# A value convolution's oldest tap as diagonal products on TensorE, and a new order by odd and even slots

## The chip, the cores and the metric

The kernel runs on one core of one Trainium2 chip, as one launch. The metric is device time in microseconds (us); the kernel before takes 1670.02 us (median of 3 runs, 1666.37 to 1673.09). The engines are TensorE (PE; its weight loads are PEld), VectorE (DVE), ScalarE (ACT), GpSimd (POOL) and SyncE (SP, which here issues DMAs). Each runs its own instructions in the order written, and they meet only at semaphores.

## The reference, cut to what matters

```python
# x: (2, 2048, 256); 16 heads of 64 channels; all float32
q, k, v = x @ Wq.T, x @ Wk.T, x @ Wv.T
q, k, v = (causal_depthwise_conv(y, w, b) for ...)  # per channel: b + sum over 4 taps w[tap] * y[t - 3 + tap]
g, beta = log_sigmoid(x @ Wg.T), sigmoid(x @ Wb.T)
k = k / norm(k);  q = q / 8
# per token and head, in order of time (gated delta rule):
#   Sk = S^T k;  S = exp(g) * S + beta * k (v - Sk)^T;  o = S^T q
x = layernorm(x + o @ Wo.T)
x = layernorm(x + routed_experts(x) + shared_expert(x))   # 64 experts, 6 a token
```

The change touches only the convolution of v and the order of the work on the delta rule.

## The kernel before, in words

Three phases follow each other: the gates (to about 57 us), the delta rule (to about 1120 us) and the mixer with its experts. The change is in the delta rule.

**Macros and slots.** The delta rule is cut into 64 macros (`NM`): one pair of heads and a span of 256 tokens, of both sequences. A macro holds 4 chunks of 64 tokens. A loop of 71 slots (`SLOTS`) is written out by hand for every engine; slot t works on several macros at once: macro t (`m`) is projected, macro t-1 (`before`) is convolved, turned and multiplied, macro t-5 (`mi`) has its triangular matrix inverted, and the chain over time (the state S) of a group of two macros advances by two steps, `one` and `two_`. A group's four steps take two slots, so odd and even slots differ: odd slots hold step 0, which needs the finished inverse, and the start of the small 16x16 inverses (`begin_blocks`, `join_fours`), even slots their end (`join_eights`).

**Values.** The projected values land in one PSUM bank `p_j`. ACT copies them to `hist` (channels on partitions, 3 older tokens ahead of each 64) and writes tap 3 and the bias into `yv` (`last_tap`, L796). DVE adds taps 2, 1 and 0 with `conv_values` (L615), each a scalar-times-tensor-plus-tensor over 128x512; each adds one to the semaphore `conv_v`. PE then turns `yv` into tokens on partitions with transposes (`turn_values`, L432), for chunks 0 and 1 and, after `chain_update` and `exponents`, for chunks 2 and 3; `turned` tells ACT, which squares the keys (L810, for DVE's `lengths`, L632) and copies keys and values on (L813).

**Inverse.** Four products in `p_i` (all L464 on PE) alternate with DVE's subtractions `horner` (L703): `inverse_r`, `inverse_rx`, `inverse_ry1`, `inverse_ry2`. The last `horner` is `tt_out`; `inverse_r` of the next macro and the step 0 of the chain wait for it. `inverse_r` also waits for `xd`, which comes by way of a store to memory and a load back (L333, L342, L347 on SP).

**Chain.** `chain_state` (L498, L508), DVE `residual` (L711), `chain_solve` (L523), ACT `solved` (L825), `chain_update` (L535, L544), DVE `update` (L719). `products` (L455) fills all of `p_xy`, and DVE's `mask` (L644) reads it.

**Order around the change.** On PE a slot begins with `chain_state` and the key projection and ends with the query projection, `inverse_ry1`, `products`, `inverse_ry2`. On DVE it begins with the last `horner` of the previous slot's macro, then `residual`, value taps 1 and 0, query taps 2 and 1, `update`, query tap 0, `gate`, `lengths`; it ends with `update`, key taps, value tap 2, `horner`, `mask`.

Of the kernel before, what the change touches and what calls it, by code (L numbers as in the profile page):

```python
# [14 lines left out]
NPAIR = H // 2  # L15
NTOK = NB * T
NTILE = NTOK // 128
C = 64
# [7 lines left out]
CH = 3 + C  # L26
HIST = 8 * CH
# [1 line left out]
RUN = PIECES * C  # L29
UNIT = C // SUB * LANE  # L30
REGION = 32 * UNIT
WCOLS = 2 * 3 * 128
E, K, CAP, I = 64, 6, 128, 176
IA, IB = 112, 64
SI = 2 * I
# [9 lines left out]
def view(t, offset, *dims, parts=None):  # L45
    row = t[:, :].ap[0][0]
    first, count = parts or (0, t.shape[0])
    return bass.AP(t, first * row + offset, [[row, count], *[list(d) for d in dims]])


def half(i):
    return (64 * i, 64)
# [161 lines left out]
def delta_phase(nc, a, s):  # L214
# [5 lines left out]
    with ExitStack() as own:  # L220
# [14 lines left out]
        yv = two("yv", 512)  # L235
# [36 lines left out]
        def is_macro(m):  # L272
            return 0 <= m < NM
# [121 lines left out]
        def _(pe):  # L395
            def project(m, n, done):
                e = m % 2
                if n == 1 and m == 0:
                    pe.wait_ge(tap_k, 1)
                if n == 1 and m >= 1:  # L400
                    pe.wait_ge(exped, m)
                if n == 2:
                    pe.wait_ge(tap_v, m + 1)
                if n == 0:
                    if m >= 1:
                        pe.wait_ge(tap_q, m)
                    pe.wait_ge(w_in[e], 16 * (m // 2 + 1))
                    if m % NPAIR == 0:
                        pe.wait_ge(xt_in[m // 8 % 2], 16 * (m // 16 + 1))
                for ch in range(2):  # L410
                    mm = pe.matmul(p_j[:, :], w[e][:, (ch * 3 + n) * 128:(ch * 3 + n) * 128 + 128],  # L411
                                   xt[m // 8 % 2][:, ch * 512:ch * 512 + 512], start=ch == 0, stop=ch == 1)
                mm.then_inc(done, 1)
# [12 lines left out]
            def turn_values(m, chunks):  # L426

                e = m % 2
                pe.wait_ge(conv_v, 3 * m + 3)
                for c in chunks:  # L430
                    for h in range(2):
                        mm = pe.transpose(view(p_xy, h * 512 + 256 + c * C, (1, C)), view(yv[e], c * 128, (1, 128), parts=half(h)),  # L432
                                          view(const, C_ID + 64 * h, (1, C), parts=half(h)))
                if chunks[-1] == 3:
                    mm.then_inc(turned, 1)

# [113 lines left out]
            for t in range(SLOTS):  # L550
                m, before, mi = t, t - 1, inverse_macro(t)
                one, two_ = chain_step(t, 0), chain_step(t, 1)
                if one:
                    chain_state(*one)
                if is_macro(m):
                    project(m, 0, proj_k)
                if one:
                    chain_solve(*one)
                if is_macro(before):
                    turn_keys(before)  # L560
                    turn_values(before, (0, 1))
                if one:
                    chain_update(*one)
                if is_macro(before):
                    exponents(before)
                if is_macro(before):
                    turn_values(before, (2, 3))
                if is_macro(mi):
                    inverse_r(mi)
                if two_:  # L570
                    chain_state(*two_)
                if is_macro(m):
                    project(m, 1, proj_v)
                if two_:
                    chain_solve(*two_)
                if is_macro(mi):
                    inverse_rx(mi)
                if two_:
                    chain_update(*two_)
                if is_macro(m):  # L580
                    project(m, 2, proj_q)
                if is_macro(mi):
                    inverse_ry1(mi)
                if is_macro(before):
                    products(before)
                if is_macro(mi):
                    inverse_ry2(mi)

        @block.vector
        def _(ve):  # L590
# [14 lines left out]
            def conv_values(m, tap):  # L605

                e = m % 2
                out = view(yv[e], 0, (C, 8), (1, C))
                if tap == 2:
                    ve.wait_ge(carried, m + 1)  # L610
                    ve.wait_ge(tap_v, m + 1)
                else:
                    ve.wait_ge(conv_v, 3 * m + 2 - tap)
                column = (m % NPAIR * 3 + 2) * (TAPS + 1) + tap
                ve.scalar_tensor_tensor(out, view(hist[e], HIST + tap, (CH, 8), (1, C)),  # L615
                                        cw[:, column:column + 1], out, ALU.mult, ALU.add).then_inc(conv_v, 1)
# [106 lines left out]
            for t in range(SLOTS):  # L723
                m, before, mi = t, t - 1, inverse_macro(t)
                one, two_ = chain_step(t, 0), chain_step(t, 1)
                small_group = (t - 3) // 2
                odd, even = t % 2 == 1 and 0 <= small_group < NG, t % 2 == 0 and 0 <= small_group < NG
                if is_macro(mi - 1):
                    horner(mi - 1, ry2_done, 48, tt_out)
                if one:  # L730
                    residual(*one)
                if is_macro(before):
                    conv_values(before, 1)
                    conv_values(before, 0)
                    conv(before, 1, tap_q, conv_q, (2, 1))
                if one:
                    update(*one)
                if is_macro(before):
                    conv(before, 1, tap_q, conv_q, (0,))
                    gate(before)  # L740
                    lengths(before)
                if even:
                    join_eights(small_group, 0, "products")
                if is_macro(m) and t % 2:
                    conv(m, 0, tap_k, conv_k, (2,))
                if is_macro(before):
                    inverse_lengths(before)
                if two_:
                    residual(*two_)
                if even:  # L750
                    join_eights(small_group, 0, "sums")
                    join_eights(small_group, 1, "products")
                    join_eights(small_group, 1, "sums")
                if is_macro(m) and t % 2:
                    conv(m, 0, tap_k, conv_k, (1, 0))
                if odd:
                    begin_blocks(small_group)
                    join_fours(small_group)
                if is_macro(m) and t % 2 == 0:
                    conv(m, 0, tap_k, conv_k, (2,))  # L760
                if is_macro(mi):
                    horner(mi, rx_done, 16, y1_out)
                if two_:
                    update(*two_)
                if is_macro(m) and t % 2 == 0:
                    conv(m, 0, tap_k, conv_k, (1, 0))
                if is_macro(m):
                    conv_values(m, 2)
                if is_macro(mi):
                    horner(mi, ry1_done, 32, y2_out)  # L770
                if is_macro(before):
                    mask(before)

        @block.scalar
# [145 lines left out]
        def _(po):  # L920
# [56 lines left out]
            for t in range(SLOTS):  # L977
                m, before, mi = t, t - 1, inverse_macro(t)
                one, two_ = chain_step(t, 0), chain_step(t, 1)
                if is_macro(before):  # L980
                    po.wait_ge(conv_v, 3 * before + 1)
                if one:
                    decay_state(*one)
                if is_macro(mi):
                    off_diagonal(mi)
                if is_macro(m):
                    carry_in(m)
                if is_macro(before):
                    carry_out(before)
                if is_macro(t - 2):  # L990
                    roots(t - 2)
                if is_macro(before):
                    po.wait_ge(gated, before + 1)
                if two_:
                    decay_state(*two_)
                if is_macro(before):
                    clip(before)
                    factors(before)
                    if t % 2 and t >= 3:
                        po.wait_ge(inverted, STEPS * ((t - 3) // 2) + 11)  # L1000
                    if t % 2 == 0 and is_macro(m):
                        po.wait_ge(conv_k, 3 * m + 1)
                    weight(before)
# [664 lines left out]
```

## Time and profile before

| | |
|---|---|
| profiled execution, whole | 1670.89 us |
| its span, first to last instruction | 1669.1 us |
| PE busy | 1459.8 us (87%) |
| DVE busy | 1202.0 us (72%) |
| ACT busy | 895.3 us (54%) |
| POOL busy | 808.5 us (48%) |
| DVE, L615, value taps, x192 | 150.9 us, 786 ns of one |
| DVE, L602, key and query taps, x384 | 294.8 us, 768 ns of one |
| mean granted TensorE clock | 0.959 of 2.4 GHz |

The shares are averages over three phases with different limits. In the delta rule alone both PE and DVE are busy for over nine tenths of the time. A matmul's end is modelled, so its busy time hides short waits; starts are exact. Each float32 matmul of the program is two instructions (a transpose one), so a call with 8 products shows as x16. "<-" names the instruction that ended an engine's wait.

### The profile page before, as it was taken

To read this page: it belongs to the slowest core of one execution; us is meant where nothing else is said; L and a number is where in the kernel's file an instruction comes from. 1 tells how busy PE (TensorE), PEld (TensorE's weight loads), DVE (VectorE), ACT (ScalarE), POOL (GpSimd) and SP (SyncE) were. 2 spreads that over 40 slices of the span, in tenths; PEclk is the share of its full clock that TensorE was granted. 3 is DMA by queue.
4 is the path that set the end of the run, shared out by engine and by line. 5 is a ranking of instruction groups with operands and counts; after the bars stand their busy time and mean duration, and the time that the engine had idled before them with its cause. 6 is when DMAs were issued, how large, how long until landed. Compare 5 with 4: busy or idle time off the path is not lost. (4 is left out here: it accounts for less than half of the span.)

```text
span 1669.1 us, 62375 instructions
## 1 busy us (share of the span) xinstructions
PE 1459.8 (87%) x25360; PEld 1060.4 (64%) x25360; DVE 1202.0 (72%) x2714; ACT 895.3 (54%) x2506; POOL 808.5 (48%) x1042
## 2 busy tenths in 40 slices
PE   6678999999999999999999999759999997988970
PEld 6235666666666666666666666658899986766650
DVE  1589999999999999998989999524666664323325
ACT  1367777777777777876777777310111110323333
POOL 1133444344344344344334344213777777777775
PEclk9879999999999999999999999788999999999995
DMA  8335555565655655655655565427666521899658
GB/s 321 91 80 119 130 121 128 142 124 131 138 121 134 137 120 134 138 117 131 140 119 128 128 122 127 93 67 228 187 177 187 181 72 37 237 255 254 122 85 309
DMA packets 529133, 242.69 MB, mean 145 GB/s; under 512 B 430000, under 2 KB 495536, under 8 KB 527952
## 3 DMA queue, kind: packets, MB, share of 16 engines
q1 hardware_dynamic: 376176, 198.43, 44.4%
q10 hardware_dynamic: 134208, 21.25, 7.0%
q0 software_dynamic: 18464, 19.03, 6.4%
q8 instruction: 201, 3.29, 0.8%
q14 instruction: 84, 0.69, 0.1%
HBM read 167.13 MB, written 71.50 MB: 143 GB/s over the span
## 5 line engine op out<-in xcount | busy, mean ns | idle before, releaser
L411 PE MATMUL delta_p_j<-xt,w 128*128 128x512 f32 x768 | 395.2, 638 | 22.6 <-ACT delta_yv L796 8.6
L602 DVE SCALAR_TENSOR_TENSOR delta_kq<-delta_hist,cw,delta_kq 128x512 f32<-128x512 f32 x384 | 294.8, 768 | 15.5 <-ACT delta_kq L796 10.6
L973 POOL TENSOR_TENSOR delta_sd<-state,eg_end 128x256 f32<-128x256 f32 x128 | 79.9, 624 | 385.2 <-DVE delta_kqg L625 252.4
L786 ACT ACTIVATE delta_hist<-delta_p_j 128x512 f32<-128x512 f32 x192 | 115.5, 602 | 222.1 <-PE delta_p_j L411 218.7
L411 PEld LDWEIGHTS delta_p_j<-xt,w 128*128 128x128 f32 x768 | 134.3, 195 | 141.9 <-issue 104.5
L1486 POOL DMA_INDIRECT slot_tokens<-tokens,mix_slot x192 | 190.0, 989 | 61.8 <-issue 52.5
L960 POOL TENSOR_TENSOR ex<-ex,delta_bp 128x512 f32<-128x512 f32 x64 | 68.0, 1063 | 188.5 <-DVE delta_xi L682 110.7
L615 DVE SCALAR_TENSOR_TENSOR delta_yv<-delta_hist,cw,delta_yv 128x512 f32<-128x512 f32 x192 | 150.9, 786 | 5.2 <-ACT delta_yv L796 2.9
L857 ACT ACTIVATE delta_kpv<-delta_kpv,delta_root 128x64 f32<-128x64 f32 x512 | 137.2, 360 | 0.0
L523 PEld LDWEIGHTS delta_p_c<-delta_r,delta_kkq 64*64 64x64 f32 x2048 | 71.5, 137 | 102.6 <-issue 52.7
L851 ACT ACTIVATE delta_kpv<-delta_kpv,delta_fk 128x64 f32<-128x64 f32 x512 | 129.0, 346 | 0.0
L464 PEld LDWEIGHTS delta_p_i<-delta_kkq,rt 64*32 64x32 f32 (+1 forms) x4096 | 67.6, 100 | 92.0 <-DVE delta_kkq L703 88.4
L1390 DVE SCALAR_TENSOR_TENSOR wo<-wo,mix_p_h 112x256 f32<-112x256 f32 x64 | 27.0, 421 | 136.2 <-ACT wo L1448 131.1
L1253 PE MATMUL mix_p_h<-wo,w 128*112 128x128 f32 (+1 forms) x768 | 101.9, 283 | 18.9 <-ACT wo L1442 18.6
L1253 PEld LDWEIGHTS mix_p_h<-wo,w 128*112 128x112 f32 (+1 forms) x768 | 89.6, 183 | 42.4 <-ACT wo L1442 36.5
L1509 POOL DMA_INDIRECT acc<-mix_ot,mix_places x64 | 100.6, 1572 | 31.3 <-issue 17.8
L464 PE MATMUL delta_p_i<-delta_kkq,rt 64*32 64x32 f32 (+1 forms) x4096 | 81.5, 184 | 32.5 <-DVE delta_kkq L703 32.5
L967 POOL TENSOR_TENSOR delta_root<-delta_n,half_power 128x8 f32<-128x8 f32 x64 | 106.6, 1666 | 0.0
L1416 ACT ACTIVATE mix_es<-mix_p_g,mix_negmax 128x64 f32<-128x64 f32 x32 | 10.1, 314 | 176.6 <-DVE mix_negmax L1316 176.6
L796 ACT ACTIVATE delta_kq<-delta_p_j,cw 128x512 f32<-128x512 f32 x128 | 100.3, 783 | 0.0
L523 PE MATMUL delta_p_c<-delta_r,delta_kkq 64*64 64x64 f32 x2048 | 89.1, 227 | 10.2 <-DVE delta_r L711 7.3
L644 DVE TENSOR_TENSOR delta_kkq<-delta_p_xy,ex 128x1024 f32<-128x1024 f32 x64 | 78.2, 1222 | 22.9 <-PE delta_p_xy L455 21.9
(171 smaller groups left out, 3345.7 us busy)
## 6 DMA issues: line engine op xcount, KB each, us to landing
delta_xd<-x_scratch SPq DMA_DIRECT2D x256, 128.0 KB
w<-in_wqkv SPq DMA_DIRECT2D x64, 384.0 KB, 3.8
w<-in_w SPq DMA_DIRECT2D x64, 352.0 KB, 3.8
delta_eg<-eg_rows SPq DMA_DIRECT2D x128, 130.0 KB, 3.0
n_scratch<-delta_kkq ACTq DMA_DIRECT2D x128, 128.0 KB, 3.1
ot<-o SPq DMA_DIRECT2D x128, 128.0 KB, 3.0
xt<-ot SPq DMA_DIRECT2D x8, 1024.0 KB
mix_ot<-ot SPq DMA_DIRECT2D x8, 1024.0 KB
```

The source lines that it names most:

```text
L411: mm = pe.matmul(p_j[:, :], w[e][:, (ch * 3 + n) * 128:(ch * 3 + n) * 128 + 128], xt[m // 8 % 2][:, ch * 512:ch * 512 + 512], start=ch == ...
L464: mm = pe.matmul(view(p_i, g * C + first, (1, count), parts=(64 * sh, rows)), view(lhs, g * C, (1, rows), parts=half(sh)), view(rhs, at + ...
L523: mm = pe.matmul(view(p_c, h * 512 + 128 + q * C, (1, C), parts=half(b)), view(kkq, ring(group * 2 + q) + h * 256 + c * C, (1, C), parts=h ...
L602: ve.scalar_tensor_tensor(out, view(hist[e], i * 2 * HIST + tap, (CH, 8), (1, C)), cw[:, column:column + 1], out, ALU.mult, ALU.add).then_ ...
L615: ve.scalar_tensor_tensor(out, view(hist[e], HIST + tap, (CH, 8), (1, C)), cw[:, column:column + 1], out, ALU.mult, ALU.add).then_inc(conv ...
L786: ac.activation(view(hist[e], n * HIST + 3, (CH, 8), (1, C)), view(p_j, 0, (C, 8), (1, C)), ACT.Copy)
L851: ac.activation(kpv[:, at:at + C], kpv[:, at:at + C], ACT.Copy, scale=fk[:, g:g + 1]).then_inc(kp_out, 1)
L857: ac.activation(kpv[:, at:at + C], kpv[:, at:at + C], ACT.Copy, scale=root[m % 2][:, g:g + 1]).then_inc(vp_out, 1)
L967: po.tensor_tensor(root[m % 2][:, :], n2[:, :], view(s.half_power, 0, (0, 8)), ALU.pow).then_inc(small, 1)
L1253: mm = pe.matmul(p_h[e % 2][0:count, to:to + 128], s.w13[:, at * 704 + ch * SI + first:at * 704 + ch * SI + first + count], xbt[e % 2][:, ...
L1486: po.indirect_dma_start(out=s.tok.ap(), out_offset=bass.IndirectOffsetOnAxis(ap=slot[i % 2][:, k:k + 1], axis=0), in_=tokens[:, i:i + 1], ...
L1509: po.indirect_dma_start(out=s.acc[e % 2].ap(), out_offset=bass.IndirectOffsetOnAxis(ap=places[:, e:e + 1], axis=0), in_=yb[e % 4], in_offs ...
```

## The change

- DVE's value tap 0 goes: `conv_values(before, 0)` is not called, and `conv_v` counts 2 a macro.
- PE does it instead. The weights of tap 0 come as two 64x64 diagonal matrices in 64 more columns of the projection weights (`WCOLS` 768 to 832). After the transposes of two chunks, 8 products of `hist` (as stationary operand, shifted to tap 0) with the diagonal accumulate on the turned values in PSUM.
- `inverse_ry2` moves from the end of a slot to the next slot: ahead of the key projection in odd slots, behind it in even ones.
- `products` goes ahead of `inverse_ry1` in odd slots.
- On DVE the last `horner` moves behind `residual` (odd) or behind query taps 2 and 1 (even); query tap 0 moves ahead of `update`; `mask` goes ahead of the second `horner` in odd slots.

```diff
-WCOLS = 2 * 3 * 128
+WCOLS = 2 * 3 * 128 + C
...
             def turn_values(m, chunks):
-                pe.wait_ge(conv_v, 3 * m + 3)
+                pe.wait_ge(conv_v, 2 * m + 2)
                 for c in chunks:
                     for h in range(2):
-                        mm = pe.transpose(view(p_xy, h * 512 + 256 + c * C, (1, C)), view(yv[e], c * 128, (1, 128), parts=half(h)),
-                                          view(const, C_ID + 64 * h, (1, C), parts=half(h)))
+                        pe.matmul(view(p_xy, h * 512 + 256 + c * C, (1, C)), view(yv[e], c * 128, (1, 128), parts=half(h)),
+                                  view(const, C_ID + 64 * h, (1, C), parts=half(h)), is_transpose=True, start=False, stop=False,
+                                  skip_group_check=True)
+                for c in chunks:
+                    for b, h in QUADS:
+                        mm = pe.matmul(view(p_xy, h * 512 + 256 + c * C, (1, C), parts=half(b)),
+                                       view(hist[e], HIST + (c * 2 + b) * CH, (1, C), parts=half(h)),
+                                       view(w[e], 768, (1, C), parts=half(h)), start=False, stop=True, skip_group_check=True)
...
 # PE, a slot
                     chain_state(*one)
+                if is_macro(mi - 1) and t % 2:
+                    inverse_ry2(mi - 1)
                 if is_macro(m):
                     project(m, 0, proj_k)
+                if is_macro(mi - 1) and t % 2 == 0:
+                    inverse_ry2(mi - 1)
...
                     project(m, 2, proj_q)
+                if is_macro(before) and t % 2:
+                    products(before)
                 if is_macro(mi):
                     inverse_ry1(mi)
-                if is_macro(before):
+                if is_macro(before) and t % 2 == 0:
                     products(before)
-                if is_macro(mi):
-                    inverse_ry2(mi)
...
 # DVE, a slot
-                if is_macro(mi - 1):
-                    horner(mi - 1, ry2_done, 48, tt_out)
                 if one:
                     residual(*one)
+                if is_macro(mi - 1) and t % 2:
+                    horner(mi - 1, ry2_done, 48, tt_out)
                 if is_macro(before):
                     conv_values(before, 1)
-                    conv_values(before, 0)
                     conv(before, 1, tap_q, conv_q, (2, 1))
+                if is_macro(mi - 1) and t % 2 == 0:
+                    horner(mi - 1, ry2_done, 48, tt_out)
+                if is_macro(before):
+                    conv(before, 1, tap_q, conv_q, (0,))
                 if one:
                     update(*one)
                 if is_macro(before):
-                    conv(before, 1, tap_q, conv_q, (0,))
                     gate(before)
...
+                if is_macro(before) and t % 2:
+                    mask(before)
                 if is_macro(mi):
                     horner(mi, ry1_done, 32, y2_out)
-                if is_macro(before):
+                if is_macro(before) and t % 2 == 0:
                     mask(before)
```

The waits of `conv_values` and of POOL on `conv_v` are renumbered from 3 to 2 a macro.

## Rows read from the trace of the kernel before

**Rows 1.** Starts (us) of DVE's gate instruction L625, one a slot, 127 to 1048 us.

```profile
L625 DVE TENSOR_TENSOR delta_kqg<-delta_kq,delta_eg x60: 1224/1225/1226, 127.3 to 1046.6; 128x1024 f32<-128x1024 f32 x60
```

**Rows 2.** Busy us (x instructions): PE, PEld, DVE, ACT, POOL; clock, DMA share, GB/s.

```profile
127.00:1048.00 921.00, 866.86 (x20415) 577.10 (x20411) 856.99 (x1623) 702.55 (x1977) 378.71 (x587) 0.99 0.58 128
```

**Rows 3.** Who waited for whom, 127 to 1048 us: us in total, times, longest.

```profile
PE delta_p_i L464 <- DVE delta_kkq L703: 27.4, 49, 0.9
DVE delta_kkq L644 <- PE delta_p_xy L455: 14.8, 30, 0.7
DVE state L719 <- PE delta_p_c L535: 12.6, 32, 0.7
PE delta_p_i L464 <- DMA delta_xd<-x_scratch: 9.3, 10, 1.3
```

**Rows 4.** Line L615 on DVE, 127 to 1048 us: ns shortest/median/longest.

```profile
L615 DVE SCALAR_TENSOR_TENSOR delta_yv<-delta_hist,cw,delta_yv x177: 744/752/1292, 134.7 to 1043.3; 128x512 f32<-128x512 f32 x177
```

**Rows 5.** Timeline of DVE in an even slot: start us, us, engine, line, [idle before].

```profile
601.58 1.23 DVE L644 TENSOR_TENSOR delta_kkq<-delta_p_xy,ex 128x1024 f32<-128x1024 f32 x1 [0.59 <-PE delta_p_xy L455]
...
603.25 1.53 DVE L615 SCALAR_TENSOR_TENSOR delta_yv<-delta_hist,cw,delta_yv 128x512 f32<-128x512 f32 x2
...
608.50 0.68 DVE L632 TENSOR_REDUCE delta_n<-delta_sq 128x8 f32<-128x512 f32 x1
...
616.53 1.22 DVE L644 TENSOR_TENSOR delta_kkq<-delta_p_xy,ex 128x1024 f32<-128x1024 f32 x1
```

**Rows 6.** Timeline of PE over an even slot and the end of an odd one.

```profile
600.31 1.10 PE L455 MATMUL delta_p_xy<-delta_kq 64*64 64x128 f32 x32
601.34 0.57 PE L464 MATMUL delta_p_i<-delta_kkq,rt 64*16 64x16 f32 x32
...
602.47 1.98 PE L411 MATMUL delta_p_j<-xt,w 128*128 128x512 f32 x4
604.38 0.68 PE L523 MATMUL delta_p_c<-delta_r,delta_kkq 64*64 64x64 f32 x16
604.99 0.46 PE L423 MATMUL delta_p_xy<-const,delta_kq 64*128 64x64 f32 x8
...
605.55 0.46 PE L535 MATMUL delta_p_c<-delta_u,delta_kpv 64*64 64x64 f32 x16
605.83 0.41 PE L544 MATMUL delta_p_d<-delta_kkq,delta_u 64*64 64x64 f32 x16
606.38 0.38 PE L445 MATMUL delta_p_j<-arg_r,arg_l 118*128 118x512 bf16 x1
...
615.06 1.10 PE L455 MATMUL delta_p_xy<-delta_kq 64*64 64x128 f32 x32
616.66 0.49 PE L464 MATMUL delta_p_i<-delta_kkq,rt 64*16 64x16 f32 x26 [0.50 <-DVE delta_kkq L703]
...
623.82 1.98 PE L411 MATMUL delta_p_j<-xt,w 128*128 128x512 f32 x4
625.92 0.68 PE L523 MATMUL delta_p_c<-delta_r,delta_kkq 64*64 64x64 f32 x16
...
630.57 0.69 PE L464 MATMUL delta_p_i<-delta_kkq,rt 64*32 64x32 f32 x32 [0.65 <-DVE delta_kkq L703]
```

**Rows 7.** Timeline of ACT in the even slot.

```profile
605.46 0.78 ACT L796 ACTIVATE delta_kq<-delta_p_j,cw 128x512 f32<-128x512 f32 x1
...
607.55 0.60 ACT L810 ACTIVATE delta_sq<-delta_p_xy 128x512 f32<-128x512 f32 x1
```

**Rows 8.** Timeline of SP's queue: the store of the small inverses, the load back.

```profile
612.59 0.39 SPq L333 DMA_DIRECT2D x_scratch<-delta_xi  x1
617.37 1.28 SPq L342 DMA_DIRECT2D delta_xd<-x_scratch  x2
```

**Rows 9.** Timeline of PE where `xd` is late.

```profile
779.32 1.18 PE L464 MATMUL delta_p_i<-delta_xd,noff 64*64 64x48 f32 x29 [1.30 <-DMA delta_xd<-x_scratch]
```

**Rows 10.** The 5 us after it, columns as in rows 2.

```profile
780.00:785.00 5.00, 5.00 (x74) 3.09 (x69) 4.62 (x14) 2.16 (x8) 1.38 (x4) 0.66 0.52 87
```

**Rows 11.** Timeline of PE in the last slots, which hold chain and inverse alone.

```profile
1083.75 0.57 PE L464 MATMUL delta_p_i<-delta_kkq,rt 64*16 64x16 f32 x32 [0.52 <-DVE delta_kkq L703]
```

More of the change, by code:

```diff
@@ L612, in conv_values @@
                 else:
-                    ve.wait_ge(conv_v, 3 * m + 2 - tap)
+                    ve.wait_ge(conv_v, 2 * m + 2 - tap)
                 column = (m % NPAIR * 3 + 2) * (TAPS + 1) + tap
@@ L980, in _ @@
                 if is_macro(before):
-                    po.wait_ge(conv_v, 3 * before + 1)
+                    po.wait_ge(conv_v, 2 * before + 1)
                 if one:
@@ L1637 @@
                    .reshape(NPAIR, 128, TAPS + 1) for n in "kqv"])
+    diag = np.zeros((NPAIR, 2, C, C), np.float32)
+    diag[:, :, np.arange(C), np.arange(C)] = g["attn_cv_w"][:, 0, 0].reshape(NPAIR, 2, C)
     left, right = exponent_operands()
@@ L1644 @@
         "wg": f(wg),
-        "wqkv": f(wqkv),
+        "wqkv": f(np.concatenate([wqkv, diag.reshape(NPAIR, 128, C)], 2)),
         "x": f(x),
```

## The prediction

> **What bounds the kernel now.** I read the page's busy shares first, then the delta rule alone, since nothing outside it changes. One instruction a slot gives the length of a slot: 60 starts of DVE's gate from 127.3 to 1046.6 us, so 919.3 / 59 = 15.58 us [rows 1]. In that stretch DVE is busy for 857 of 921 us and PE for 867 [rows 2]: 93% and 94%. Neither is far from the bound, so the question is which one waits for which. The table of waits shows both [rows 3]. DVE waits 14.8 us for `products` ahead of `mask` and 12.6 us for the state products ahead of `update`, 27.4 us in 59 slots, 0.46 us a slot. What is left, 15.58 - 0.46 = 15.12 us a slot, is DVE's own content: instructions and the hand-overs between them. One slot agrees: from `mask` at 601.58 to `mask` at 616.53 are 14.95 us in which DVE waits for nobody [rows 5]. So even slots are bound by DVE.
>
> PE shows 27.4 us of waits for `horner` and 9.3 us for the late `xd`, 0.62 us a slot [rows 3]. This is too little, since a modelled matmul end covers the first part of a wait. By starts: from `products` to `inverse_ry2` are 1.03 us where nothing is late (600.31 to 601.34) and 1.60 us where `horner` is (615.06 to 616.66), a wait of 0.57 us beside the 0.50 shown [rows 6]. The same correction of 0.07 us on the 0.65 us ahead of `inverse_ry1` (630.57) gives 0.72 us. Smaller ones show in no wait row: from a projection to `chain_solve` are 2.10 us (623.82 to 625.92) against 1.91 (602.47 to 604.38), so 0.19 us for `residual`; and from `chain_update`'s second half to the exponents are 0.55 us (605.83 to 606.38), where 16 matmuls of that kind take 0.28 (605.55 to 605.83) [rows 6]; of the other 0.27 I take 0.12 as a wait for ACT's `last_tap`, which ends at 606.24 [rows 7], in each slot, and as much for `solved`. An odd and an even slot thus hold 0.57 + 0.72 + 0.19 + 4 x 0.12 = 1.96 us, 0.98 us a slot with `xd` (0.16) partly in it or beside it; I take 1.03. PE's content is 15.58 - 1.03 = 14.55 us. PE is 0.57 us below DVE now. PE's waits are mostly for a late DVE, DVE's for PE's tail: the two hold each other up at the slot's end.
>
> **The change part by part.** *Value tap 0 leaves DVE.* One of three L615 of a slot goes, 0.75 us [rows 4]; two run in 1.53 us [rows 5]. DVE's content becomes 15.12 - 0.75 = 14.37 us.
>
> *Diagonal products come to PE.* Two calls a slot, each 8 products of 64x64 with 64 columns, x16 in the trace. The same shape, with both halves of rows and columns in turn as here, is L535: 16 start within 0.28 us (605.55 to 605.83). The same shape in L523's order, where neighbours share the array half by half, takes 0.61 us (604.38 to 604.99) [rows 6]. The change uses L535's kind of order, so I take 0.28 a call, 0.56 us a slot. Below: the transposes already hand over to 64x64 matmuls, so part of a hand-over may be saved, 0.45 us a slot. Above: 1.22 us a slot, L523's price.
> The Trainium skill speaks against this price: the page "TensorE: Matmul & The Clock Gate", section "Wait — 56ns, not 53.3ns?", says that matmul starts are never closer than about 25 ns however few the columns. By it 16 would take 0.40 us and the slot 0.80, which would take back 14 of the microseconds gained below. The rows show 0.28 us for 16, 17.5 ns each [rows 6]; the trace disagrees, and the trace decides.
>
> PE's content becomes 14.55 + 0.56 = 15.11 us. PE passes DVE (14.37) and becomes the bound. Without the reordering little would be won: 15.11 plus the old waits would be a slower slot than before.
>
> *`inverse_ry2` goes to the next slot.* The same 32 instructions, 0.50 us. Its `horner` now has `chain_state` (0.63 us, 601.84 to 602.47, of which the rows show the end) and in even slots also a projection (1.91 us) as cover, where it had `products` alone and fell short by 0.57 us. With DVE 0.75 us earlier relative to PE, I lay two slots out: `horner` ends 0.3 us or more ahead of PE in both. This wait goes. What is queued behind `inverse_ry2` is later by 0.50 us: in even slots `chain_solve`, so ACT's `solved` and `last_tap`, so the exponents; PE reaches them after 0.61 + 0.30 + 0.55 + 0.28 x 2 us more work of its own, about when ACT is done. I leave 0.1 us there.
>
> *`products` ahead of `inverse_ry1` in odd slots.* It fills the 0.72 us of wait for the `horner` behind `join_fours` with 1.04 us of work that is ready (the queries have been convolved for long). This wait goes too.
>
> *DVE's moves.* `residual` first serves `chain_solve`; the 0.19 us goes. Query tap 0 ahead of `update` uses up 0.73 us that `update` would wait for `chain_update`. New waits on DVE: `lengths` needs the squares (L810), which need `turned`, which is now two calls later, 0.56 us, and in even slots 0.50 more. Before, `lengths` starts at 608.50 and the squares end at 608.15 [rows 5, 7]. In the layout DVE waits 0.35 us there, and for `products` ahead of `mask` 0.2 us. Behind them are queued `join_eights` and the next `residual`. DVE has 15.11 - 14.37 = 0.74 us to spare, so this costs nothing on the path; were the cover gone, it would cost 0.2 us a slot (first rival).
>
> *`xd`.* It is stored after `join_eights` (612.59) and loaded 4.8 us later (617.37) [rows 8]; `inverse_r` is at 622.3. In the layout the store is 0.3 us later and `inverse_r` 0.85 us later from the even slot's start, so the margin grows by 0.5 us. Of 0.16 us a slot I keep 0.08. Where it was 1.30 us late, the granted clock fell to 0.66 in the 5 us behind, i.e. to 1.2 GHz for part of them [rows 9, 10]; this should be seen less. SP's queue is otherwise in the same order; `turned`, for which it waits ahead of loading weights, is a microsecond later, with nine to spare. The weights are 416 instead of 384 KB, a load with as much room: no cost.
>
> *Ramp and end.* Before 127 us slots go by the one bank `p_j` between PE and ACT; nothing gained, nothing lost. After 1048 us `inverse_ry2` behind `chain_state` covers its 0.52 us [rows 11] about as often as `horner` comes later for the chain: between -2 and +2 us, I take 0.
>
> **The sum.** A slot: 15.11 + 0.08 (`xd`) + 0.06 left for ACT and hand-overs = 15.25 us. 59 slots x (15.58 - 15.25) = 19.5 us. The profiled execution took 1670.9 us (span 1669.1), so 1651.4; the median of the runs lies 0.9 below it, so 1650.5, and I forecast **1651 us**.
>
> **The rivals.**
> *ACT takes the wait's place.* PE waits for ACT's tap and exponentials and DVE for the squares, both now behind a later `turned`. For: ACT is busy for 702 of 921 us [rows 2], and in even slots from the key projection to the value projection without a pause. Against: 0.7 us of slack on DVE. At 0.2 us a slot more, 15.45: 1651 + 12 = 1663 us.
> *All of it comes off.* `xd` is never late, the clock doesn't fall, products cost 0.45: the slot is 15.05 us, 59 x 0.53 = 31 us, 1639 us.
> *Slower: PE is the bound, and the products cost as much as L523.* Place: both calls of `turn_values`; price 1.22 us a slot. The slot is 14.55 + 1.22 + 0.14 = 15.91 us, 59 x 0.33 = 19 us more, 1690 us. It decides from 0.89 us a slot on, since 14.55 + 0.89 + 0.14 = 15.58. For: PE is now the bound, so everything added counts in full, a clock at 1.2 GHz too. Against: the row of L535. In part (1.0 to 1.1 us) it gives some 1678 to 1684.
>
> **Chances.** Forecast 0.53 (1644 to 1658), ACT's wait 0.20, all of it 0.15, slower 0.12. Faster by over 0.5% (8 us; about what a measurement tells from no change) is the first and third, 0.68; within 0.5% the second, 0.20; slower 0.12. The range for 8 in 10 takes in the second case and most of the third: 1639 to 1671.
>
> **What would show it.** Right: 2 L615 a slot; the diagonal products as x16 rows about 0.28 us to the next start; no wait of L464 for L703 worth 0.1 us a slot; PE without gaps, DVE with 0.6 to 0.8 us of waits, ahead of L632 and L644; slots of 15.2 to 15.3 us. Wrong: 16 products over 0.45 us; slots of 15.4 with waits of PE for L796 or L804; or DVE still without waits, which would mean that PE wasn't the bound.

## The result and the profile after

The changed kernel takes 1626.28 us (median of 4 runs, 1622.26 to 1629.23) against 1668.28 us (4 runs); the ratio is 0.9742, with a 95% interval of 0.9711 to 0.9774. It is 42 us faster. Forecast were 1651 us, 19 us faster, with a range of 1639 to 1671: the direction was right, the size was half of what came, and the time lies below the range.

The profiled execution took 1626.23 us, its span 1624.4 against 1669.1 us. The gate instruction, one a slot, shows where the 44.7 us are; its line of after answers to [rows 1] (ns shortest/median/longest, first and last start).

```profile
L635 DVE TENSOR_TENSOR delta_kqg<-delta_kq,delta_eg x60: 1216/1218/1225, 122.2 to 1003.8; 128x1024 f32<-128x1024 f32 x60
```

Slots went from 15.58 to (1003.8 - 122.2) / 59 = 14.94 us: 59 x 0.64 = 37.6 us. The ramp ahead of it is 127.3 - 122.2 = 5.1 us shorter, what follows the last gate (622.5 against 620.6) 1.9 us.

In the busy shares of that stretch (columns as in [rows 2]) PE goes from 94 to 99%, which fits PE as the bound. DVE's share hardly moves, from 93 to 92%, though it has a tap less to do.

```profile
127.00:1003.00 876.00, 868.83 (x22181) 599.33 (x22179) 808.97 (x1555) 694.04 (x1960) 386.37 (x583) 1.00 0.62 137
```

Who waited for whom in after, 127 to 1010 us (us in total, times, longest); it answers to [rows 3], which ends at the last gate in the same way.

```profile
DVE delta_n L642 <- ACT delta_sq L824: 20.1, 56, 0.5
DVE state L729 <- PE delta_p_c L541: 13.1, 28, 0.8
DVE delta_kkq L654 <- PE delta_p_xy L461: 9.7, 36, 1.0
PE delta_p_i L470 <- DMA delta_xd<-x_scratch: 2.0, 4, 0.6
PE delta_p_i L470 <- DVE delta_kkq L713: 1.4, 2, 0.8
```

PE's waits for `horner` fell from 27.4 to 1.4 us and those for `xd` from 9.3 to 2.0. DVE now waits for the squares, as laid out in the prediction, and still for `chain_update` ahead of `update`.

The timeline of PE over an even slot of after, from `products` of the odd one to `products` of the even one, then the end of the slot (start us, us, engine, line, operation).

```profile
607.49 1.10 PE L461 MATMUL delta_p_xy<-delta_kq 64*64 64x128 f32 x32
608.52 0.69 PE L470 MATMUL delta_p_i<-delta_kkq,rt 64*32 64x32 f32 x32
609.15 0.46 PE L504 MATMUL delta_p_c<-state,delta_kqg 64*64 64x64 f32 x16
...
609.77 1.98 PE L411 MATMUL delta_p_j<-xt,w 128*128 128x512 f32 x4
611.69 0.57 PE L470 MATMUL delta_p_i<-delta_kkq,rt 64*16 64x16 f32 x32
612.19 0.68 PE L529 MATMUL delta_p_c<-delta_r,delta_kkq 64*64 64x64 f32 x16
...
613.10 0.29 PE L432 MATMUL delta_p_xy<-const,delta_yv 64*128 64x64 f32 x4
613.32 0.46 PE L437 MATMUL delta_p_xy<-w,delta_hist 64*64 64x64 f32 x16
613.60 0.41 PE L541 MATMUL delta_p_c<-delta_u,delta_kpv 64*64 64x64 f32 x16
613.83 0.41 PE L550 MATMUL delta_p_d<-delta_kkq,delta_u 64*64 64x64 f32 x16
...
618.47 0.68 PE L529 MATMUL delta_p_c<-delta_r,delta_kkq 64*64 64x64 f32 x16
618.99 1.02 PE L470 MATMUL delta_p_i<-delta_xd,rt 64*64 64x48 f32 x29
...
620.48 1.98 PE L411 MATMUL delta_p_j<-xt,w 128*128 128x512 f32 x4
622.40 0.69 PE L470 MATMUL delta_p_i<-delta_kkq,rt 64*32 64x32 f32 x32
623.02 1.10 PE L461 MATMUL delta_p_xy<-delta_kq 64*64 64x128 f32 x32
623.95 0.41 PE L504 MATMUL delta_p_c<-state,delta_kqg 64*64 64x64 f32 x16
```

No row has a wait in brackets, where [rows 6] has two. The 16 diagonal products take 0.28 us to the next start (613.32 to 613.60), as priced. The even slot, from one `chain_state` (609.15) to the next (623.95), is 14.80 us of PE's own work: PE is the bound, at less than the 15.11 us that the prediction gave it.

### The profile page after: what moved, and what is told of

The parts are those of the page before. It is cut to its first block and busy times, and to the rows that moved or that the text cites. A ratio compares the mean times of both kernels' runs of the same rounds, so it can differ in the third digit from the quotient of the medians.

```text
span 1624.4 us, 66407 instructions
## 1 busy us (share of the span) xinstructions
PE 1469.7 (90%) x27408; PEld 1091.4 (67%) x27408; DVE 1157.5 (71%) x2650; ACT 895.3 (55%) x2506; POOL 819.7 (50%) x1042
## 5 line engine op out<-in xcount | busy, mean ns | idle before, releaser
L411 PE MATMUL delta_p_j<-xt,w 128*128 128x512 f32 x768 | 386.9, 627 | 22.5 <-ACT delta_yv L810 8.8
L981 POOL TENSOR_TENSOR delta_root<-delta_n,half_power 128x8 f32<-128x8 f32 x64 | 115.9, 1812 | 0.0
L625 DVE SCALAR_TENSOR_TENSOR delta_yv<-delta_hist,cw,delta_yv 128x512 f32<-128x512 f32 x128 | 103.6, 810 | 2.9 <-ACT delta_yv L810 2.8
L1208 PEld LDWEIGHTS mix_p_h<-mix_x1t,mix_ws 128*128 128x128 f32 x768 | 93.7, 197 | 2.0
L1208 PE MATMUL mix_p_h<-mix_x1t,mix_ws 128*128 128x128 f32 x768 | 93.6, 280 | 0.0
```

Of the source, the lines that this page charges most:

```text
L981: po.tensor_tensor(root[m % 2][:, :], n2[:, :], view(s.half_power, 0, (0, 8)), ALU.pow).then_inc(small, 1)
L1208: mm = pe.matmul(dst[:, piece * 128:piece * 128 + 128], wt[:, ch * SP3 + piece * 128:ch * SP3 + piece * 128 + 128], x1t[i % NXT][:, ch * 1 ...
```

## The experiments

Fifteen kernels ran on three chips, each beside the kernel before on its own chip. On two of the chips every kernel takes some 85 us more (before: 1756 and 1749 us, on the third 1667), nearly all of it behind the delta rule: on one of the two the changed kernel has its last gate at 1006.1 us and its end at 1704.4, where the profile above has 1003.8 and 1624.4. So times are compared within a chip, and slots across chips.

| kernel | us | before beside it | ratio (95%) | mean slot |
|---|---|---|---|---|
| tap on PE, old order | 1756.1 | 1756.2 | 0.9997 (0.9976 to 1.0018) | 15.58 |
| new order, tap on DVE | 1723.9 | 1756.2 | 0.9824 (0.9778 to 0.9870) | 15.00 |
| old order, no tap 0 at all | 1755.4 | 1756.2 | 0.9996 (0.9968 to 1.0024) | 15.52 |
| after, no products | 1721.3 | 1756.2 | 0.9808 (0.9760 to 0.9857) | 14.99 |
| after, products twice | 1760.5 | 1756.3 | 1.0023 (0.9998 to 1.0047) | 15.72 |
| after, products in pairs | 1713.2 | 1756.3 | 0.9753 (0.9701 to 0.9804) | 14.98 |
| after, `inverse_ry2` at the end | 1763.7 | 1756.3 | 1.0037 (1.0012 to 1.0063) | 15.74 |
| after, `products` last | 1715.5 | 1756.3 | 0.9753 (0.9708 to 0.9798) | 15.04 |
| after again | 1708.1 | 1749.2 | 0.9753 (0.9713 to 0.9792) | 14.99 |
| before, `inverse_ry2` moved | 1732.4 | 1749.2 | 0.9892 (0.9849 to 0.9936) | 15.37 |
| after, DVE's order back | 1745.8 | 1749.2 | 0.9984 (0.9959 to 1.0009) | 15.57 |
| after, `lengths` wait filled | 1712.0 | 1749.2 | 0.9766 (0.9730 to 0.9803) | 15.01 |
| before, key tap cut | 1647.0 | 1667.4 | 0.9886 (0.9859 to 0.9913) | 15.13 |
| before, value tap cut | 1667.3 | 1667.4 | 1.0003 (0.9983 to 1.0024) | 15.53 |
| after, key tap cut | 1625.6 | 1667.4 | 0.9744 (0.9708 to 0.9780) | 15.00 |

The mean slot is the mean of the 59 gaps between 60 gate instructions of the profiled execution, as above. Where the text gives medians, "even slots" are the gaps from an even slot's gate to the next gate, "odd slots" those from an odd slot's. The ratio is estimated from all runs of both kernels and can differ a little from the quotient of the medians.

**The tap alone, in the old order.** The diff of `turn_values`, `conv_v` and the weights, without the moves.

```diff
-                        mm = pe.transpose(view(p_xy, h * 512 + 256 + c * C, (1, C)), view(yv[e], c * 128, (1, 128), parts=half(h)),
+                        pe.matmul(view(p_xy, h * 512 + 256 + c * C, (1, C)), view(yv[e], c * 128, (1, 128), parts=half(h)),
...
+                for c in chunks:
+                    for b, h in QUADS:
+                        mm = pe.matmul(view(p_xy, h * 512 + 256 + c * C, (1, C), parts=half(b)),
...
-                    conv_values(before, 0)
```

> The order of before, with tap 0 on TensorE as diagonal products. Theory A (PE's own content was 14.3 us a slot before and not 14.55; PE's waits for DVE came from DVE being late, so 0.75 us less on DVE and 0.52 us more on PE cover them in any order): slots of 15.0 to 15.1 us, 1633 to 1640 us. Rival B (the new order takes the waits away and the tap alone only moves the bound to PE): PE keeps its 0.6 to 0.7 us waits ahead of inverse_ry1 and inverse_ry2, slots of 15.3 to 15.5, 1655 to 1668 us.

Nothing: 15.58 us a slot, as before. Theory A fails. Rival B is the nearer one, but even it expected 15.3 to 15.5 us a slot.

**The order alone.** All the moves, with `conv_values(before, 0)` still on DVE; the diff is against the changed kernel.

```diff
-                        pe.matmul(view(p_xy, h * 512 + 256 + c * C, (1, C)), view(yv[e], c * 128, (1, 128), parts=half(h)),
+                        mm = pe.transpose(view(p_xy, h * 512 + 256 + c * C, (1, C)), view(yv[e], c * 128, (1, 128), parts=half(h)),
...
-                for c in chunks:
-                    for b, h in QUADS:
-                        mm = pe.matmul(view(p_xy, h * 512 + 256 + c * C, (1, C), parts=half(b)),
...
+                    conv_values(before, 0)
```

> The order of after, with tap 0 on DVE as before. Theory A: DVE with its content of 15.1 us a slot stays the bound, only its 0.46 us of waits can go, so 15.2 us a slot and 1645 to 1655 us. Rival B: most of the gain is here, 1630 to 1640 us.

32 us faster, 15.00 us a slot: 0.58 of the 0.64 us. Rival B again. DVE still does everything that it did in before, in less than the 15.12 us a slot that the prediction took for its content. It now waits for only 10 us in 59 slots; the two largest parts are these (127 to 1012 us):

```profile
DVE delta_kkq L648 <- PE delta_p_xy L455: 5.3, 8, 2.0
DVE delta_n L636 <- ACT delta_sq L819: 3.4, 11, 0.6
```

So some 14.8 us a slot are DVE's own work in this order. Two things above all made it look longer in before. About 0.08 us a slot were parts of waits for PE that show as no wait. And query tap 0 stood right ahead of `gate`, which reads what it writes: there 0.88 us pass from start to start (before, even slot), where the same tap hands over to `update` after 0.66 us in even slots of the new order.

```profile
606.48 0.75 DVE L602 SCALAR_TENSOR_TENSOR delta_kq<-delta_hist,cw,delta_kq 128x512 f32<-128x512 f32 x1
607.36 1.23 DVE L625 TENSOR_TENSOR delta_kqg<-delta_kq,delta_eg 128x1024 f32<-128x1024 f32 x1
```

**The old order without tap 0 on any engine.**

```diff
-                pe.wait_ge(conv_v, 3 * m + 3)
+                pe.wait_ge(conv_v, 2 * m + 2)
...
-                    conv_values(before, 0)
```

> The order of before, tap 0 of the values left out altogether (nobody computes it). It shows what 0.75 us less on DVE brings without any price on PE. Theory A: PE at 14.3 us and DVE at 14.4 us of content, slots of 14.6 to 14.8, 1610 to 1625 us. Rival B: the waits at the slot's end stay, 15.0 or more, 1640 us.

Again nothing (15.52). The timeline of DVE, two slots' `update` and what stands between, shows where the 0.75 us went.

```profile
606.65 0.42 DVE L719 TENSOR_TENSOR state<-delta_sd,delta_p_c 128x256 f32<-128x256 f32 x1 [0.70 <-PE delta_p_c L535]
...
616.70 0.41 DVE L703 TENSOR_TENSOR delta_kkq<-delta_xd,delta_p_i 128x256 f32<-128x256 f32 x1
...
622.05 0.42 DVE L719 TENSOR_TENSOR state<-delta_sd,delta_p_c 128x256 f32<-128x256 f32 x1 [1.16 <-PE delta_p_c L535]
```

And PE's timeline in the same kernel:

```profile
617.17 0.57 PE L464 MATMUL delta_p_i<-delta_kkq,rt 64*16 64x16 f32 x32 [0.50 <-DVE delta_kkq L703]
617.67 0.46 PE L498 MATMUL delta_p_c<-state,delta_kqg 64*64 64x64 f32 x16
...
618.29 1.98 PE L411 MATMUL delta_p_j<-xt,w 128*128 128x512 f32 x4
620.21 0.68 PE L523 MATMUL delta_p_c<-delta_r,delta_kkq 64*64 64x64 f32 x16
...
621.46 0.46 PE L535 MATMUL delta_p_c<-delta_u,delta_kpv 64*64 64x64 f32 x16
```

This is a loop over both engines. DVE's `update` at 606.65 is followed by 10.46 us of DVE work in its queue, to the end of `horner` at 617.11; PE's `inverse_ry2` waits for it (617.17), and behind it in PE's queue stand the state products, a projection, `chain_solve`, the turns and `chain_update`, for whose end DVE's next `update` waits (622.05). 10.46 + 4.94 = 15.40 us, the period of the slot, with no wait inside either stretch. The next slot, an odd one, has a loop too, but it closes one product earlier, at `inverse_ry1`, whose `horner` is late behind `begin_blocks` and `join_fours`:

```profile
630.48 0.55 DVE L703 TENSOR_TENSOR delta_kkq<-delta_xd,delta_p_i 128x384 f32<-128x384 f32 x1
631.08 0.70 PE L464 MATMUL delta_p_i<-delta_kkq,rt 64*32 64x32 f32 x32 [0.65 <-DVE delta_kkq L703]
637.54 0.42 DVE L719 TENSOR_TENSOR state<-delta_sd,delta_p_c 128x256 f32<-128x256 f32 x1 [0.70 <-PE delta_p_c L535]
```

From `update` (622.05) to the end of that `horner` (631.03) are 8.98 us of DVE, from there to the next `update` 6.51 us of PE's part: 15.49. The value taps are in neither loop: DVE does them while PE goes through its part. Taken away, they leave a wait ahead of `update`, which here is 55.6 us in 57 slots against 12.6 in before [rows 3].

**After without the products** (transposes as in before; tap 0 left out).

```diff
-                for c in chunks:
-                    for b, h in QUADS:
-                        mm = pe.matmul(view(p_xy, h * 512 + 256 + c * C, (1, C), parts=half(b)),
...
```

> After without the diagonal products (tap 0 of the values is left out). If PE is the bound in after, all of the products' price comes back until DVE (14.37 us a slot) is met: 14.4 to 14.5 us a slot, 1598 to 1606 us. If the products lie beside waits (rival C: after is not bound by PE), nothing comes back: 1620 to 1626 us.

Neither: slots are 14.65 us on the median in even slots against 14.74, so 0.1 us comes back before something else binds (DVE waits for the squares, 27.2 us). The mean is no better (14.99): PE now waits 7.6 us for the weights' load where it waited 0.9 in after, and 8.8 us for `xd` where it waited 2.0. On the whole the products cost nothing that these runs can tell; the ratios' intervals overlap.

**After with the products twice** (the loop over `QUADS` is repeated).

```diff
+                for c in chunks:
+                    for b, h in QUADS:
+                        mm = pe.matmul(view(p_xy, h * 512 + 256 + c * C, (1, C), parts=half(b)),
...
```

> After with each diagonal product issued twice (tap 0 counts double). If PE is the bound, one more set costs its full price, 2 x 0.24 us a slot by L541's starts in after (16 in 0.24 us), 64 x 0.47 = 30 us: 1656 us. If PE has slack, under 15 us. If the second set costs over 0.3 us a call, products cost more than the rows of before show.

The undisturbed even slot is 15.21 us against 14.74 (medians), 0.47 us more, the priced 2 x 0.24. The mean slot is 0.73 us longer, and 1760.5 against 1713 us is 47 us, not 30. The rest are disturbances: PE idles for the profile's "issue" (waiting for nothing that it shows) for up to 1.5 us at a time.

```profile
PE delta_p_i L475 <- issue: 7.5, 12, 1.3
PE delta_p_xy L442 <- issue: 3.8, 4, 1.5
PE delta_p_j L411 <- DMA w<-in_wqkv: 3.0, 4, 1.5
```

What ends those pauses was not settled.

**Products in pairs.**

```diff
-                for c in chunks:
-                    for b, h in QUADS:
+                for quads in (((0, 0), (1, 1)), ((0, 1), (1, 0))):
+                    for c in chunks:
+                        for b, h in quads:
```

> After with the products in an order in which only two quarters of the array are at work at a time, as in chain_solve (L529). By that row 16 take 0.61 us in place of 0.28, 64 x 2 x 0.33 = 42 us if PE is the bound: 1668 us. This is the price on which the slower rival rested. If the order doesn't matter: 1626 us.

A miss: the order doesn't matter. PE's timeline of this kernel has the 16 in 0.28 us as well.

```profile
601.70 0.47 PE L438 MATMUL delta_p_xy<-w,delta_hist 64*64 64x64 f32 x16
601.98 1.02 PE L471 MATMUL delta_p_i<-delta_xd,noff 64*64 64x48 f32 x29
```

`chain_solve` puts all its 16 on two quarters of the array (rows and columns of the same half), 8 on each. It takes 0.61 us where transposes follow [rows 6] and 0.52 where products of its own kind do (after: 618.47 to 618.99); here it is 4 on each of four, in 0.28. That fits a cost by how many fall on one quarter, some 0.07 us each, and not by which follow each other; the first half is read from these rows and wasn't tried by itself. The slower rival rested on a price that these products have in neither order.

**`inverse_ry2` back at the slot's end** (both new calls out, the old one in).

```diff
-                if is_macro(mi - 1) and t % 2:
-                    inverse_ry2(mi - 1)
...
-                if is_macro(mi - 1) and t % 2 == 0:
-                    inverse_ry2(mi - 1)
...
+                if is_macro(mi):
+                    inverse_ry2(mi)
```

> After with inverse_ry2 back at the end of the slot. Theory A (DVE is early enough now): a wait of 0.1 to 0.3 us in some slots, 1628 to 1640 us. Rival B (the new place is needed): in odd slots inverse_ry1 and inverse_ry2 stand side by side, with horner between them, over 0.6 us every second slot, 1645 to 1655 us.

The whole gain is gone, 50 us with it (15.74 us a slot; odd slots 16.27 on the median). Rival B, and more: with `mask` now ahead of `horner` in odd slots, the loop holds 1.2 us more of DVE.

**`products` last in odd slots, `mask` behind `horner`.**

```diff
-                if is_macro(before) and t % 2:
-                    products(before)
...
-                if is_macro(before) and t % 2 == 0:
+                if is_macro(before):
...
-                if is_macro(before) and t % 2:
-                    mask(before)
...
-                if is_macro(before) and t % 2 == 0:
+                if is_macro(before):
```

> After with products behind inverse_ry1 and mask behind horner in odd slots too, as before. In before this place held a wait of 0.72 us every second slot. Theory A: DVE is 0.75 us earlier relative to PE's work, so the wait is nearly gone, 1626 to 1634 us. Rival B: 0.5 us or more every second slot comes back, 16 us: 1642 us.

Theory A's size: 15.04 against 14.99 us, 1715.5 us against 1713.2 for the pairs. This move is worth nothing that can be told, once the tap has left DVE.

**The changed kernel again.**

> The changed kernel itself, beside the others on their chip: slots of 14.9 us on the mean and 14.74 to 14.91 on the median as in its first profile. If a chip takes longer after the delta rule, this kernel and before take it alike: 40 to 44 us faster than before.

41 us, as expected.

**`inverse_ry2` and its `horner` moved, nothing else.** From before, with the two new calls on PE and the two new places on DVE.

```diff
+                if is_macro(mi - 1) and t % 2:
+                    inverse_ry2(mi - 1)
...
+                if is_macro(mi - 1) and t % 2 == 0:
+                    inverse_ry2(mi - 1)
...
-                if is_macro(mi):
-                    inverse_ry2(mi)
...
-                if is_macro(mi - 1):
-                    horner(mi - 1, ry2_done, 48, tt_out)
...
+                if is_macro(mi - 1) and t % 2:
+                    horner(mi - 1, ry2_done, 48, tt_out)
...
+                if is_macro(mi - 1) and t % 2 == 0:
+                    horner(mi - 1, ry2_done, 48, tt_out)
```

> The order of before and tap 0 on DVE; only inverse_ry2 and its horner are moved to their new places. Theory D (a loop bounded before: horner ahead of inverse_ry2, then on PE inverse_ry2, state, projection, solve, turns, update, then DVE's update and all of DVE's work down to that horner; 4.8 us on PE and 10.5 us on DVE): the loop is cut here, slots of 15.0 to 15.15 us, 25 to 33 us faster than before. Rival A (each engine's own content is the bound): DVE keeps its 15.1 us, under 10 us faster.

17 us faster, 15.37 us a slot. Even slots fall to 14.94 us (median), which is DVE's own work without a wait; odd ones stay at 15.48. DVE waits for `chain_update` only once, for 0.7 us, where it was 12.6 us in before, so both loops are open. What is left in odd slots is a shorter hand-over: `inverse_ry1` waits for its late `horner`, and `mask` for the `products` behind it.

```profile
DVE delta_kkq L646 <- PE delta_p_xy L455: 14.7, 29, 0.7
```

The order as a whole gives 0.37 us a slot more than this. `products` ahead of `inverse_ry1` takes that wait away (5.3 us are left with the order alone), and query tap 0 no longer stands right ahead of `gate`. How the 0.37 us divide between the two wasn't tried. Theory D's size was too large here, rival A's too small.

**DVE's order back.**

```diff
+                if is_macro(mi - 1):
+                    horner(mi - 1, ry2_done, 48, tt_out)
                 if one:
                     residual(*one)
-                if is_macro(mi - 1) and t % 2:
-                    horner(mi - 1, ry2_done, 48, tt_out)
...
+                    conv(before, 1, tap_q, conv_q, (0,))
                     gate(before)
```

> After, with DVE's first horner ahead of residual again and query tap 0 behind update again. In even slots residual now stands behind a horner that waits for inverse_ry2 behind the projection; chain_solve comes 0.5 us behind inverse_ry2 and needs residual, so PE waits about 0.7 us every second slot, 20 us or more slower than after. If DVE's order didn't matter (PE is the bound and DVE has 0.5 us to spare): within 5 us of after.

38 us slower than after. As expected PE waits for `residual`, and DVE for `inverse_ry2`:

```profile
DVE delta_kkq L713 <- PE delta_p_i L470: 52.5, 30, 2.6
PE delta_p_c L529 <- DVE delta_r L721: 21.1, 29, 0.9
```

The two places of `inverse_ry2`, PE's and DVE's, belong together.

**The wait for the squares filled.**

```diff
                     gate(before)
-                    lengths(before)
                 if even:
                     join_eights(small_group, 0, "products")
                 if is_macro(m) and t % 2:
                     conv(m, 0, tap_k, conv_k, (2,))
+                if is_macro(before):
+                    lengths(before)
```

> After, with join_eights' first products (even slots) or key tap 2 (odd slots) ahead of lengths, so that they fill DVE's wait of 0.35 us for the squares. PE is the bound, so undisturbed slots stay at 14.74 and 14.91 us; the store of the small inverses is 0.35 us earlier, which takes away part of the late xd (the mean slot is 0.12 us above the median): 2 to 5 us faster than after. If DVE's wait doesn't matter at all: the same as after.

The same as after (1712.0 against 1708.1, intervals overlapping). But the edit did not fill the wait, it moved it. `lengths` no longer waits for the squares; the step behind it waits for GpSimd, which comes after `lengths`, by as much in all:

```profile
DVE delta_rn L646 <- POOL delta_n L962: 21.1, 58, 0.4
```

So this run doesn't show what DVE's idle time is worth; the last experiment does.

**The same cut inside the loop and outside it.** In before, DVE's tap 0 of the keys (between `update` and `horner`) or of the values (ahead of `update`) is computed for 1 of 64 tokens.

```diff
+                    n = 1 if (i, tap) == (0, 0) else C
+                    cut = view(kq[e], i * 512, (C, 8), (1, n))
```

> The kernel before, with DVE's key tap 0 computed for one token of each chunk only (8 columns for 512; the rest of that tap is left out). About 0.6 us less on DVE, at a place inside the loop of theory D (between update and the horner ahead of inverse_ry2). Theory D: the slot loses most of it in odd slots, where key tap 0 stands between begin_blocks and residual, and in even slots too: 0.3 to 0.6 us a slot, 20 to 35 us faster than before. Theory C (only each engine's content counts, and DVE is not the bound): as with the value tap, nothing.

```diff
+                n = 1 if tap == 0 else C
+                cut = view(yv[e], 0, (C, 8), (1, n))
```

> The kernel before, with DVE's value tap 0 cut in the same way. The same 0.6 us less on DVE, but ahead of update, beside PE's part of the loop. Theory D: update then waits for PE instead, within 5 us of before. Theory A (DVE's content is the bound): as fast as the key tap's cut, 20 us or more.

The key tap's cut gives 20.4 us and 0.45 us a slot, the value tap's 0.1 us and 0.05. The gates of the first:

```profile
L627 DVE TENSOR_TENSOR delta_kqg<-delta_kq,delta_eg x60: 1224/1225/1227, 125.0 to 1017.4; 128x1024 f32<-128x1024 f32 x60
```

In the second the time turns up as a wait, as in the kernel without tap 0:

```profile
DVE state L721 <- PE delta_p_c L535: 40.4, 58, 1.2
PE delta_p_i L464 <- DVE delta_kkq L705: 29.5, 52, 0.7
```

Same engine, same kind of instruction, the same time taken away (each cut tap takes 0.23 us in place of 0.75): what counts is whether it stands in the loop. Theory D is shown.

**The key tap cut in after.**

```diff
+                    n = 1 if (i, tap) == (0, 0) else C
+                    cut = view(kq[e], i * 512, (C, 8), (1, n))
```

> After, with the key tap 0 cut. If PE is the bound in after and the loop is open, 0.6 us less on DVE brings nothing: 40 to 46 us faster than before, as after is. If a loop through DVE still binds in after, 15 us or more beyond that.

1625.6 us against 1667.4, as after itself stands to before: 0.5 us less on DVE brings nothing. The loop is open, and PE is the bound.

## Why the prediction was right or wrong

*What bounds the kernel: wrong, and this is the step that failed.* It took each engine's time without waits for its own content, 15.12 us on DVE and 14.55 on PE, and the larger for the bound. Before was bound by a loop over both, 10.5 us of DVE and 4.9 of PE in turn in one slot, 9.0 and 6.5 in the other. The even slot without a wait on DVE [rows 5] was a tie: the value taps filled almost exactly the time in which PE went through its part of the loop. With the tap cut, and nobody computing it, both contents are below 14.6 us by the prediction's own count, and the slot still takes 15.52; a wait of 55.6 us has come.

*The tap's 0.75 us off DVE: right in size, wrong in effect.* Alone it is worth 0. In the new order it is worth 15.00 - 14.94 = 0.06 us a slot at most, and some 9 us in all: the ratio goes from 0.9824 to 0.9753, where the intervals overlap. It is so little because the order alone is bound by DVE at some 14.8 us a slot, and after by PE, which has the products, at 14.80. Part of the 9 us is the ramp: the first of the 60 gates is at 125.0 us with the order alone and at 122.2 in after. The prediction gave the ramp and the end 0; they brought 5.1 and 1.9 us.

*The products' price: right for a call by itself.* 0.28 us a call was forecast and read; what they add to a slot is less, as the next point shows. A floor of 25 ns from start to start, which the Trainium skill gives ("TensorE: Matmul & The Clock Gate", "Wait — 56ns, not 53.3ns?"), would make it 0.40 us; the trace has 0.28 / 16 = 17.5 ns, and the measurement decides.

*PE's content: mis-sized.* 14.55 + 0.56 = 15.11 us was forecast. The even slot of after is 14.80 without a wait, and the two medians are 14.74 and 15.00. The 0.31 us has two parts. Added up row by row, PE's work in before is about 14.46 us: its waits there come to some 1.1 us a slot with `xd` counted in full, where 1.03 were taken. That is 0.1 us. The other 0.2 us is the 0.56 added on top, which came to about 0.34 net, since neighbours in the new kernel hand over sooner: `chain_update`'s first half takes 0.23 us (613.60 to 613.83) for 0.28 [rows 6], and `products`, now followed by `chain_state`, 0.93 (623.02 to 623.95) for 1.03. The price of the second set of products, 0.47 us for two calls, says the same; the prediction had 0.45 only as its lower case. Together with the disturbances' 0.14 us the forecast slot was 15.25 against 14.94, 18 us in 59 slots, and the ramp and the end make up the other 7 of the 25 us. The 18 us is the term that put the time outside the range.

*The moves: right in place, too small in words.* "This wait goes", for both, is what after shows (1.4 us left of 27.4). But the sum booked them as what keeps the tap's gain alive. It is the other way round: the order is the gain, and the products are nearly free beside it. The statement that without the reordering the slot would be slower than before was too dark: it was 15.58 both times.

*DVE's new waits: right, but for one.* 0.35 us ahead of `lengths` (20.1 us in 56 slots) and some 0.2 for `mask` (9.7 in 36) came as laid out. The wait ahead of `update`, which query tap 0 was to use up, stayed: 13.1 us in 28 slots, against 12.6 in 32 before. They cost nothing that can be told: with 0.5 us a slot less to do, DVE waits longer and the time is the same.

*`xd`: right in direction, the cause not shown.* 9.3 us of waits became 2.0 in the same 59 slots, and 2.3 in the second profile of the changed kernel, less than the half that the sum kept. The granted clock was 1.00 (2.4 GHz) from 127 to 1003 us of after, where before had 0.99 on the mean. But the old order with the tap on PE has only 0.4 us of such waits, so these numbers don't tie it to the new order.

*The rivals.* The slower one is refuted twice, by 0.28 us in after and by the pairs. "All of it comes off" had 1639 us, and more came off, since its floor of 15.05 us a slot was PE's content mis-sized in the same way.

## What to carry to other kernels

When two engines with queues in order hand work to each other more than once a period, follow the hand-overs round until they close: if no wait lies inside either engine's stretch and the stretches add up to the period, only work inside the loop counts. An engine without waits is no proof that its content is the bound; cut one instruction inside the suspected loop and one outside it, and compare. Here an order that lets another engine's late answer meet independent work was worth 0.58 us a slot, and moving work off the engine that looked busiest 0.06.

## What the runs showed of the hardware

- 16 matmuls of 64x64 with 64 columns take 0.28 us to the next start over four quarters of the array, in either order, and 0.52 us over two quarters (0.61 with transposes behind).
- On DVE `gate`, which reads what query tap 0 has just written, starts 0.88 us behind it in before; `update`, which doesn't, starts 0.66 us behind the same tap in even slots of the order alone. That the reading is the reason wasn't tried by itself.
- With 16 more such pairs a slot PE has pauses of up to 1.5 us that no wait explains, some 0.3 us a slot on the mean; with the products once they are rare (2.6 us in all, 1.8 of it at L514).
- Two of three chips took some 85 us longer, nearly all of it behind the delta rule (slots of 14.94 and 14.99 us for the changed kernel). The cause is open.
